# Joint classifier: a new order for the last joins, a split output group and a store in two transfers

## What is computed

```
joint = v0 x v1 x v2 x v3                        # per row b
flat = joint.reshape(B, -1)                      # 512 x 65536
num_y_joint = einsum('bj,by->yj', flat, y_true)  # count
num_joint = sum(flat, axis=0)
prob_y_joint = clip(max(num_y_joint, 1e-6) / max(num_joint, 1e-6), 0, 1)
probs = einsum('yj,bj->by', prob_y_joint, flat)  # join; 512 x 100
```

## Time and profile before

| | |
|---|---|
| median of three executions | 540.55 us (540.05 to 541.52) |
| profiled execution | 540.03 us |
| its span, first to last instruction | 537.8 us |
| TensorE busy | 524.5 us, 98% of the span, 3072 matmuls |
| VectorE busy | 294.3 us, 55% |
| ScalarE, GpSimd busy | 41.5 us, 22.5 us |
| chain that ended last | TensorE 97%, VectorE 2% |

### The profile page before, as it was taken

How to read it: one execution, slowest core, us unless ns; L and a number is a source line. 1 busy time by engine, 2 the same in 40 slices (tenths; PEclk the granted TensorE clock), 3 DMA queues, 4 the chain that set the end, 5 groups by cost and what they waited for, 6 DMA issues and landing times.

```text
span 537.8 us, 8613 instructions
## 1 busy us (share of the span) xinstructions
PE 524.5 (98%) x3072; PEld 299.5 (56%) x3072; DVE 294.3 (55%) x757; ACT 41.5 (8%) x96; POOL 22.5 (4%) x19
## 2 busy tenths in 40 slices
PE   3999999999999999999999999999999999999996
PEld 1555555555555555555555555555555555555553
DVE  7887667654575444444467444444446444444445
ACT  6950000000110000000020000000001000000000
POOL 0000000000050000000022000000005000000000
PEclk9999999999999999999999999999999999999999
DMA  1744243340000000000000000000000000000000
GB/s 45 141 95 66 53 78 60 59 60 1 0 1 1 1 0 0 0 0 0 0 1 1 0 0 0 1 0 0 0 0 1 0 1 0 0 0 0 0 0 15
DMA packets 34624, 9.17 MB, mean 17 GB/s; under 512 B 34352, under 2 KB 34608, under 8 KB 34608
## 3 DMA queue, kind: packets, MB, share of 16 engines
q1 hardware_dynamic: 34080, 8.73, 8.8%
q10 hardware_dynamic: 528, 0.20, 0.1%
HBM read 0.34 MB, written 0.20 MB: 1 GB/s over the span
## 4 chain that ended last, share of the span: by engine, by line
PE 97%; DVE 2%; ACT 0%; DMA 0%; issue 0%; ACTq 0%; DVEq 0%
PE joined L378 16%; PE joined L379 16%; PE joined L380 16%; PE numbers L370 16%; PE numbers L372 16%; PE numbers L371 16%; DVE acc L354 1%; PE numbers L393 1%; PE numbers L396 1%; PE numbers L400 1%; DMA x<-in_r_logits_dram 0%; ACT p_hi L187 0%; DVE qf L243 0%; ACT q_hi L195 0%; DVE p L235 0%
## 5 line engine op out<-in xcount | busy, mean ns | idle before, releaser
L379 PE MATMUL joined<-r_lo,pt_hi 128*128 128x400 f16 x512 | 170.4, 333 | 0.0
L380 PE MATMUL joined<-r_hi,pt_lo 128*128 128x400 f16 x512 | 170.4, 333 | 0.0
L378 PE MATMUL joined<-r_hi,pt_hi 128*128 128x400 f16 x512 | 170.3, 333 | 0.0
L370 PE MATMUL numbers<-q_hi,p_hi 128*128 128x404 f16 x496 | 166.5, 336 | 0.0
L372 PE MATMUL numbers<-q_hi,p_lo 128*128 128x404 f16 x496 | 165.5, 334 | 0.0
L371 PE MATMUL numbers<-q_lo,p_hi 128*128 128x404 f16 x496 | 165.4, 333 | 0.0
L280 DVE TENSOR_SCALAR den<-numbers 128x4 f32<-128x4 f32 x128 | 20.7, 162 | 215.9 <-PE numbers L372 215.0
L292 DVE SCALAR_TENSOR_TENSOR r_lo<-ratio,r_hi 128x400 f16<-128x400 f32 x128 | 78.4, 612 | 4.4
L285 DVE SCALAR_TENSOR_TENSOR ratio<-numbers,inv 128x400 f32<-128x400 f32 x128 | 73.5, 574 | 4.4
L379 PEld LDWEIGHTS joined<-r_lo,pt_hi 128*128 (+1 forms) x512 | 50.0, 98 | 36.9
L378 PEld LDWEIGHTS joined<-r_hi,pt_hi 128*128 (+1 forms) x512 | 49.8, 97 | 37.0
(11 more groups left out here) (31 smaller groups left out, 62.5 us busy)
## 6 DMA issues: line engine op xcount, KB each, us to landing
pt_hi<-p_hi SPq DMA_TRANSPOSE x16, 3.1
pt_lo<-p_lo SPq DMA_TRANSPOSE x16, 3.2
labels<-in_r_y_true_dram ACTq DMA_DIRECT2D x1, 200.0 KB, 2.8
out_dram<-acc SPq DMA_DIRECT2D x1, 200.0 KB, 1.9
x<-in_r_logits_dram SPq DMA_DIRECT2D x1, 128.0 KB, 2.2
```

Of the source, the lines that this page charges most:

```text
L370: pe.matmul(out, p_at(p_hi, tile, k), q_at(q_hi, g, k), start=(k == 0), stop=False)
L378: pe.matmul(out, p_at(pt_hi, tile, k), r_hi[:, slot, :], start=first, stop=False)
L379: pe.matmul(out, p_at(pt_hi, tile, k), r_lo[:, slot, :], start=False, stop=False)
L380: last = pe.matmul(out, p_at(pt_lo, tile, k), r_hi[:, slot, :], start=False, stop=final)
```

## The change

Five edits, all about the end of the last group (the loops of groups 1 and 2 stay).

- TensorE's loop in group 3 ends one turn earlier; tiles 24 to 26 are joined in straight code, each with its count, tiles 28 to 30. Then count(31) comes ahead of join(27). join(27) closes `joined[3]` and signals `third_ready`.
- The last four joins (tiles 28 to 31) run k by k: for k = 0, 1 and 2 the four tiles' chunks in a row, which close `joined[k]`. For k = 3 they go into `numbers[0]` (v0 values 0 and 1) and then `numbers[1]` (2 and 3): two halves of 200 columns, 12 matmuls each, and each half signals `half_ready`.
- VectorE's loop in group 3 ends four steps earlier too, and the last step writes its r_hi and r_lo to a fifth slot.
- VectorE adds `joined[3]` first, then k = 0, 1, 2, then the two halves for k = 3: 20 adds and not 16.
- SyncE stores chunks 0 to 2 after 16 adds, and chunk 3 (one run of 400 bytes a partition) after 20, on semaphores of their own.

```diff
+    HA = AG // 2
-        r_hi = sb("r_hi", [LANES, SLOTS, PW], FP16)
-        r_lo = sb("r_lo", [LANES, SLOTS, PW], FP16)
+        r_hi = sb("r_hi", [LANES, SLOTS + 1, PW], FP16)
+        r_lo = sb("r_lo", [LANES, SLOTS + 1, PW], FP16)
...
+            out = probs.rearrange("(p k) y -> p k y", k=KC)
             sp.wait_ge(added, KC * AG)
-            sp.dma_start(probs.rearrange("(p k) y -> p k y", k=KC), acc[:, :, :]).then_inc(stored, 16)
+            sp.dma_start(out[:, 0:KC - 1, :], acc[:, 0:KC - 1, :]).then_inc(stored, 16)
+            sp.wait_ge(added, KC * AG + AG)
+            sp.dma_start(out[:, KC - 1:KC, :], acc[:, KC - 1:KC, :]).then_inc(stored_last, 16)
             sp.wait_ge(stored, 16)
+            sp.wait_ge(stored_last, 16)
...
+            for j in range(SLOTS):
+                make_ratios(STEPS - SLOTS + j, j, SLOTS if j == SLOTS - 1 else j)
+            def add(k, a, bank, at):
+                dve.scalar_tensor_tensor(acc[:, k, :], bank[:, at * CLASSES:(at + 1) * CLASSES],
+                                         v0f[:, k, S - AG + a:S - AG + a + 1], acc[:, k, :],
+                                         ALU.mult, ALU.add).then_inc(added, 1)
             dve.wait_ge(v0f_made, 1)
             dve.wait_ge(summed, GROUPS - 1)
-            for k in range(KC):
-                dve.wait_ge(joined_ready, (GROUPS - 1) * KC + k + 1)
+            for n, k in enumerate([KC - 1] + list(range(KC - 1))):
+                if n:
+                    dve.wait_ge(joined_ready, (GROUPS - 1) * KC + k + 1)
+                else:
+                    dve.wait_ge(third_ready, 1)
                 for a in range(AG):
                     if a:
-                        dve.wait_ge(added, k * AG + a)
-                    dve.scalar_tensor_tensor(acc[:, k, :], joined[k][:, a * CLASSES:(a + 1) * CLASSES],
...
+                        dve.wait_ge(added, n * AG + a)
+                    add(k, a, joined[k], a)
+            for a in range(AG):
+                dve.wait_ge(half_ready, a // HA + 1)
+                dve.wait_ge(added, KC * AG + a)
+                add(KC - 1, a, numbers[a // HA], a % HA)
...
             g = GROUPS - 1
-            join(g, TILES - 4, 0)
-            join(g, TILES - 3, 1)
-            pe.wait_ge(ratios_ready, g * TILES + TILES)
-            for k in range(KC):
-                join_chunk(TILES - 2, 2, k, False, False)
-                join_chunk(TILES - 1, 3, k, False, True)
+            for j in range(SLOTS - 1):
+                join(g, TILES - 2 * SLOTS + j, j)
+                count(g, TILES - SLOTS + j, j)
+            tile = TILES - SLOTS - 1
+            pe.wait_ge(ratios_ready, g * TILES + tile + 1)
+            count(g, TILES - 1, SLOTS - 1)
+            for k in range(KC - 1):
+                join_chunk(tile, SLOTS - 1, k, False, False)
+            join_chunk(tile, SLOTS - 1, KC - 1, False, True, third_ready)
+            rows = [0, 1, 2, SLOTS]
+            for k in range(KC - 1):
+                for j in range(SLOTS):
+                    if k == 0:
+                        pe.wait_ge(ratios_ready, g * TILES + TILES - SLOTS + j + 1)
+                    join_chunk(TILES - SLOTS + j, rows[j], k, False, j == SLOTS - 1)
+            for h in range(2):
+                out = numbers[h][:, 0:HA * CLASSES]
+                for j in range(SLOTS):
+                    tile = TILES - SLOTS + j
+                    ra = r_hi[:, rows[j], h * HA * CLASSES:(h + 1) * HA * CLASSES]
+                    rb = r_lo[:, rows[j], h * HA * CLASSES:(h + 1) * HA * CLASSES]
+                    pe.matmul(out, p_at(pt_hi, tile, KC - 1), ra, start=(j == 0), stop=False)
+                    pe.matmul(out, p_at(pt_hi, tile, KC - 1), rb, start=False, stop=False)
+                    last = pe.matmul(out, p_at(pt_lo, tile, KC - 1), ra, start=False, stop=(j == SLOTS - 1))
+                last.then_inc(half_ready, 1)
```

More of the change, by code:

```diff
@@ L126, in joint_classifier @@
         added = sem("added")
+        third_ready = sem("third_ready")
+        half_ready = sem("half_ready")
         stored = sem("stored")
+        stored_last = sem("stored_last")
         ek = x[:, :, :].rearrange("p (k v) s -> p k v s", v=NV)
@@ L274, in make_p_lo, with make_ratios @@
                 last.then_inc(p_ready, 2)
-            def make_ratios(step, slot):
+            def make_ratios(step, slot, r_slot=None):
+                r_slot = slot if r_slot is None else r_slot
                 dve.wait_ge(numbers_ready, step + 1)
@@ L289, in make_ratios @@
                 dve.wait_ge(ratio_made, step + 1)
-                dve.tensor_scalar(r_hi[:, slot, :], ratio[:, slot, :], UP, 0.0, ALU.min, ALU.max).then_inc(r_hi_made, 1)
+                dve.tensor_scalar(r_hi[:, r_slot, :], ratio[:, slot, :], UP, 0.0, ALU.min, ALU.max).then_inc(r_hi_made, 1)
                 dve.wait_ge(r_hi_made, step + 1)
-                dve.scalar_tensor_tensor(r_lo[:, slot, :], ratio[:, slot, :], UP, r_hi[:, slot, :],
+                dve.scalar_tensor_tensor(r_lo[:, r_slot, :], ratio[:, slot, :], UP, r_hi[:, r_slot, :],
                                          ALU.min, ALU.subtract).then_inc(ratios_ready, 1)
@@ L342, in _ @@
                     first = first + 2 * KC
-                with dve.Fori(first, (g + 1) * TILES - SLOTS + 1, SLOTS) as step:
+                end = (g + 1) * TILES - (SLOTS if g == GROUPS - 1 else 0)
+                with dve.Fori(first, end - SLOTS + 1, SLOTS) as step:
                     for j in range(SLOTS):
                         make_ratios(step + j, j)
+            for j in range(SLOTS):
[4 more added lines that the diff above has]
+                                         ALU.mult, ALU.add).then_inc(added, 1)
             dve.wait_ge(v0f_made, 1)
             dve.wait_ge(summed, GROUPS - 1)
-            for k in range(KC):
-                dve.wait_ge(joined_ready, (GROUPS - 1) * KC + k + 1)
+            for n, k in enumerate([KC - 1] + list(range(KC - 1))):
[3 more added lines that the diff above has]
+                    dve.wait_ge(third_ready, 1)
                 for a in range(AG):
                     if a:
-                        dve.wait_ge(added, k * AG + a)
-                    dve.scalar_tensor_tensor(acc[:, k, :], joined[k][:, a * CLASSES:(a + 1) * CLASSES],
-                                             v0f[:, k, S - AG + a:S - AG + a + 1], acc[:, k, :],
-                                             ALU.mult, ALU.add).then_inc(added, 1)
+                        dve.wait_ge(added, n * AG + a)
[4 more added lines that the diff above has]
+                add(KC - 1, a, numbers[a // HA], a % HA)
         @block.tensor
@@ L373, in count, with join_chunk @@
                 last.then_inc(numbers_ready, 1)
-            def join_chunk(tile, slot, k, first, final):
+            def join_chunk(tile, slot, k, first, final, ready=joined_ready):
                 out = joined[k][:, 0:PW]
@@ L381, in join_chunk @@
                 if final:
-                    last.then_inc(joined_ready, 1)
+                    last.then_inc(ready, 1)
             def join(g, tile, slot, first=False, final=False):
@@ L449, in _ @@
                         count(g, j + SLOTS, j)
-                    with pe.Fori(SLOTS, TILES - 2 * SLOTS + 1, SLOTS) as tile:
+                    end = TILES - SLOTS - (SLOTS if g == GROUPS - 1 else 0)
+                    with pe.Fori(SLOTS, end - SLOTS + 1, SLOTS) as tile:
                         for j in range(SLOTS):
```

## The result

The changed kernel takes 539.17 us (median of 8 executions, 538.07 to 539.79) against 540.5 us (8 executions, 540.05 to 541.52): ratio 0.9969, 95% interval 0.996 to 0.9978. Predicted were 538.9 us and -0.31%. The profiled execution took 539.34 us, its span 537.2.

The account below looks back on a forecast made before the run. TensorE, busy 98% of the span, was taken as the bound, and VectorE's adds once joined[0] is closed. Adds -1.44, store -0.30 and a wait +0.05 gave -1.69 us: 538.9 us from 540.55, range 538.0 to 540.2.

Parts of the forecast that it names:

- TensorE's order is free, slack 1.3 us at join(31)'s wait: In TensorE's reordered tail, ratios(31) are there 1.3 us before k = 0's tenth matmul wants them; cost nothing.
- VectorE keeps up with k = 0 to 2: VectorE's four adds for a k take 1.41 us, with 2.03 us between the closings of banks.
- The halves at 0.090, near the floor of 0.086: TensorE's last 24 matmuls of 200 columns stand 0.090 us apart; 0.086 is the floor, by columns.
- The last add 1.44 us earlier: VectorE's last add is done at 533.99 against 535.43 us, -1.44 us, with short matmuls at a pitch of 0.090.
- The store, -0.30 + 0.05: SyncE's second, 50 KB store lands after 1.6 us instead of 1.9, -0.30; one more wait costs about 0.05.
- Sum -1.69: Whole kernel: -1.44 for the adds, -0.30 for the store, +0.05 for a wait, giving -1.69 us.
- The load bound: Rival: weight loads bound the short matmuls, pitch 0.100 or more; 539.1 us, or 540.7 at 0.169; chance 0.15.
- the store without a gain: Rival: the small last store lands in 1.9 us or more; 539.15 us, or 540.05 at a landing of 2.8; chance 0.25.
- the instruction fetch: Rival: a late fetch in the straight code behind TensorE's loop stops it about 2.2 us; 541.05 us; chance 0.05.
- VectorE is late by its waits: Rival: on the last adds, waits each cost a queue piece of 0.1 us, four of them giving 539.3; chance 0.07.
- The spread: Whole-kernel time: the median was taken 0.5 us above the profiled execution; the medians' spread was half a microsecond.

Follow-up runs that it names:

- e6: The changed kernel with count(31) behind join(27) again and not ahead of it; 539.68 us, ratio 0.9983 to the kernel before.
- e2: The changed kernel without the halves: k = 3 closes last in joined[3], 16 adds, first store behind add 12; 539.33 us, ratio 0.9975.
- e5: The changed kernel with the last chunk in four quarters of 100 columns and the adds of k = 2 and 3 interleaved; 538.65 us, ratio 0.9961.
- e3: The changed kernel with half_ready waited on only before a = 0 and 2, and no wait on the add before at a = 0; 538.57 us, ratio 0.9965.
- e1: The changed kernel with one store of all four chunks behind the last of the 20 adds; 538.54 us, ratio 0.9963.
- e4: The kernel before with only the store in two transfers, chunks 0 to 2 behind add 12, chunk 3 behind add 16; 540.52 us, ratio 0.9997.
- e8: The quarters kernel with 24 matmuls of 400 columns on zeros ahead of TensorE's first wait; 537.16 us, ratio 0.9937 to the kernel before.

## Why the prediction was right, step by step

- *TensorE's order is free, slack 1.3 us at join(31)'s wait.* Right. Ratios(31) end at 525.39 + 0.57 = 525.96 in the changed trace, S + 506.53, and the tenth matmul of k = 0 starts at 527.32, 1.36 us later; TensorE shows no idle. e6 shows the other side: without the count's move 0.73 us of stop.
- *VectorE keeps up with k = 0 to 2.* Right: idle 0.46 to 0.64 before each, first add 0.04 behind a matmul's record. Worth 0.97 us alone (e2).
- *The halves at 0.090, near the floor of 0.086.* Right in kind; it was the floor itself. e5 shows why: at 100 columns the pitch is 0.044, with load records of 0.10 us that overlap. The trace of before had the evidence in the pair of loads that took 0.13 us; the 98 ns of a load's record is not the time for which it holds TensorE up. The floor's working was looser than its result: 0.0004 us for each of 200 columns is 0.080, not the 0.083 that the sum took.
- *The last add 1.44 us earlier.* It is 1.30. The term that was mis-sized is the wait on `half_ready` ahead of each of the four adds: I priced it once, at the step from half 0 to half 1, and gave the other adds the pitch of the earlier trace rows. It costs 0.07 on each, though already satisfied, 0.28 in all. With the waits as I priced them, 0.05 of these, the pitch of 0.086 would have given -1.53; the missing 0.23 makes it the -1.30 measured. (The 0.32 of e3 is not the same term: the first add gains 0.18 there and not 0.07, since without the wait on its predecessor, which the forecast had priced, it starts beside it.) For the same reason the last add is done 1.08 us behind the last matmul's record and not 0.8.
- *The store, -0.30 + 0.05.* It is -0.3 net (e1, e4): the landing of 1.5 is 0.4 shorter, in the middle of the 1.4 to 1.6 that I had for it, and the 0.49 from it to the span's end, where there were 0.44, fit the 0.05 for the second wait. Its data took 0.3, the upper end of what I allowed.
- *Sum -1.69.* It is -1.6 in the traces. The two errors, 0.14 too much on VectorE and 0.05 too little on the store, partly cancel, and that is luck. So is part of the match with the timed ratio: the medians moved by 1.33 us only, to 539.17 where I said 538.9.
- *The rivals.* The load bound is refuted (e5), the store without a gain too (e1, e4), the instruction fetch as well: no idle of TensorE behind the loop. So neither rule that I had set against the rows decided anything: a load's 107 ns did not bound a matmul (the Trainium skill, TensorE: Matmul & The Clock Gate, LDWEIGHTS; here 0.044 us each), and the rule on transfers under 512 bytes (the Trainium skill, DMA: Bandwidth & Descriptors, Specifications) did not keep the landing from falling to 1.5 us; the half rate of the data would fit it, but no run here has a store of 50 KB in longer rows to compare. That VectorE is late by its waits, to which I gave a chance of 0.07, was true beside the forecast, at 0.23 us.
- *The spread.* I took the half microsecond between the profiled execution and the median as noise. Most of it has a cause, the stretch ahead of S: S differs by 1.3 us between the traces, and in e8, where TensorE works early, five executions lie within 0.22 us.

## What to carry to other kernels

When one engine's work at the end of a kernel is released in steps, compare its time for a step with the distance between the steps: here 1.3 against 1.01 us let a queue of 2.4 us build up behind the last matmul, and regrouping the same matmuls, 2.03 apart, took 1 us off without less work anywhere. Finish the last piece in small parts in banks of their own so that one small operation is left, and keep to one wait per operation in a chain in which each waits for the one before it. Before comparing spans, put the traces on a common mark behind the start.

## What the runs showed of the hardware

- Matmuls of 400, 200 and 100 columns stand 0.169, 0.086 and 0.044 us apart, each with a weight load of its own. No bound by the load down to 100 columns. The Trainium skill (TensorE: Matmul & The Clock Gate, Back-to-back issue gap) gives the columns over 2.4 GHz and 2.5 ns, for a matmul by itself with nothing reckoned for loads; an estimate from it is 0.169, 0.086 and 0.044, and these traces show just that with a load for each. For a stream with loads that section has other figures, 131 ns at 512 columns among them, and the 0.169 us at 400 speak against it.
- A satisfied wait in front of an instruction that has another costs VectorE 0.07 us in a chain where each add waits for the one before it. Where the adds of two chunks alternate (e5), they start 0.23 us apart, the one with both waits too.
- TensorE, idle until 8.2 us, ran its first matmuls of 404 columns at a pitch of 0.337 us, that of 1.2 GHz, and went over to 0.171 at about 11.6 us in the trace of before and at about 13.8 in the changed kernel's, in the same stretch of code (from how long the groups from 11.40 and from 12.68 took). With 24 matmuls on zeros from 1.29 us on and 0.97 us of idle behind them, the first real ones ran at the pitch of 2.4 GHz, and five executions lay within 0.22 us, where nine of the kernel before lay within 1.4.
- A store of 50 KB in rows of 400 bytes landed in 1.5 us, its data moving for 0.3; 200 KB in rows of 1600 bytes landed in 1.9, the data moving for 0.65.
